# Attention of a transformer layer on one core: the last P·V products of a head issued together, its output copied out one exponential earlier, and extra matmuls of ones in the prologue

## The reference, cut to what matters

```python
qkv = x @ w_qkv + b_qkv                     # q, k, v: 16 heads of 16
q, k = rope(q), rope(k)
attn = softmax(q @ k.T / 4)                 # 2048 x 2048 for each of 4 x 16 heads
out = (attn @ v) @ w_out + b_out
x = layernorm(x + out)
gate, up = x @ w_gate.T / 127, x @ w_up.T / 127
x = layernorm(x + (silu(gate) * up) @ w_down.T / 127)
```

## Time and profile before

| | us |
|---|---|
| median of 3 runs | 2866.97 |
| the profiled execution, its own time | 2870.14 |
| its span | 2868.1 |
| PE busy | 2811.7 |
| VectorE (DVE) busy | 2702.9 |
| ScalarE (ACT) busy | 2591.9 |
| GpSimd (POOL) busy | 1416.7 |

### The profile page before, as it was taken

How to read it: one execution, slowest core, us unless ns; L and a number is a source line. 1 busy time by engine, 2 the same in 40 slices (tenths; PEclk the granted TensorE clock), 3 DMA queues, 4 the chain that set the end, 5 groups by cost and what they waited for, 6 DMA issues and landing times. The chain is left out here.

```text
span 2868.1 us, 70575 instructions
## 1 busy us (share of the span) xinstructions
PE 2811.7 (98%) x27022; PEld 862.5 (30%) x27022; DVE 2702.9 (94%) x3088; ACT 2591.9 (90%) x4778; POOL 1416.7 (49%) x4133
## 2 busy tenths in 40 slices
PE   8989999999999999999999999999999999999998
PEld 4531222222222222222222222222222222246665
DVE  7989999999999999999999999999999999947777
ACT  5756999999999999999999999999999999976555
POOL 7851444444444444444444444444444444436553
PEclk9978999999999999999999999999999999999999
DMA  5431111111111111111111111111111111233431
GB/s 194 142 116 28 36 35 36 35 36 35 35 35 35 34 35 36 35 36 36 35 35 35 36 35 35 35 35 36 35 35 36 35 35 35 70 90 92 118 96 38
DMA packets 121519, 146.56 MB, mean 51 GB/s; under 512 B 52832, under 2 KB 87520, under 8 KB 121180
## 3 DMA queue, kind: packets, MB, share of 16 engines
q1 hardware_dynamic: 120892, 142.02, 17.0%
q10 hardware_dynamic: 288, 0.01, 0.0%
HBM read 106.30 MB, written 35.13 MB: 49 GB/s over the span
## 5 line engine op out<-in xcount | busy, mean ns | idle before, releaser
L102 DVE TENSOR_REDUCE tile_max<-s_ps 128x1 f32<-128x1024 f32 (+1 forms) x2048 | 2282.4, 1185 | 8.8 <-PE s_ps L91 2.8
L1063 ACT ACTIVATE probs<-st_ps 128x512 f32<-128x512 f32 x4096 | 2202.2, 601 | 71.0 <-PE st_ps L942 41.1
L953 PE MATMUL o_ps<-probs,kept_v 128*17 128x256 f32 x16384 | 1283.1, 385 | 25.7 <-ACT sums L1032 25.7
L91 PE MATMUL s_ps<-k,q 64*128 64x512 f16 x4096 | 1266.2, 386 | 11.0 <-DVE tile_max L102 9.2
L942 PE MATMUL st_ps<-q,k 64*128 64x512 f16 x4096 | 1249.5, 382 | 1.1 <-ACT probs L1063 0.8
L1198 POOL TENSOR_TENSOR larger<-spared 128x256 f32<-128x256 f32 x1107 | 342.8, 310 | 675.6 <-ACT spared L1038 598.5
L953 PEld LDWEIGHTS o_ps<-probs,kept_v 128*17 128x17 f32 x16384 | 273.6, 95 | 852.2 <-ACT probs L1063 445.6
L942 PEld LDWEIGHTS st_ps<-q,k 64*128 64x128 f16 x4096 | 256.1, 94 | 902.0 <-ACT probs L1063 842.3
L1207 POOL TENSOR_TENSOR spared<-spared,larger 128x256 f32<-128x256 f32 x984 | 318.4, 324 | 81.9
L1200 POOL TENSOR_SCALAR larger<-larger 128x256 f32<-128x256 f32 x1107 | 261.4, 236 | 96.8
L91 PEld LDWEIGHTS s_ps<-k,q 64*128 64x128 f16 x4096 | 250.2, 94 | 50.4 <-DVE tile_max L102 46.5
(11 more groups left out here) (119 smaller groups left out, 1625.3 us busy)
## 6 DMA issues: line engine op xcount, KB each, us to landing
q<-q_parts SPq DMA_DIRECT2D x193, 128.0 KB
k<-k_parts SPq DMA_DIRECT2D x193, 128.0 KB
x_t<-in_x_t SPq DMA_DIRECT2D x16, 512.0 KB, 7.2
q_parts<-parts SPq DMA_DIRECT2D x32, 256.0 KB, 2.6
k_parts<-parts SPq DMA_DIRECT2D x32, 256.0 KB, 2.6
heads_out<-sums SPq DMA_DIRECT2D x256, 32.0 KB, 2.1
kept_v<-heads_out SPq DMA_DIRECT2D x16, 512.0 KB, 6.1
kept_v<-inverses_out SPq DMA_DIRECT2D x32, 256.0 KB
```

Of the source, the lines that this page charges most:

```text
L91: mm = pe.matmul(s["s_ps"][g % 2][:, j * BANK:(j + 1) * BANK], s["q"][h % 2][rows, r // KW * P:(r // KW + 1) * P], s["k"][h % 2][rows, at: ...
L102: dve.tensor_reduce(s["tile_max"][h % 2][:, r // KW, r % KW:r % KW + 1], s["s_ps"][g % 2][:, columns], AX.X, ALU.max).then_inc(s["s_read"], 1)
L953: mm = pe.matmul(o_ps[c * 32:c * 32 + VM, at:at + HALF], t["kept"][:, h, kt, :], probs[(h * KT + kt) % RING][:, c * BANK + at:c * BANK + a ...
L1063: act.activation(probs[(h * KT + kt) % RING][:, c * BANK:(c + 1) * BANK], st_ps[n % ST][:, :], ACT.Exp, scale=scale).then_inc(exp_done, 1)
```

## The change

`LAST_V = 1` replaces `ODD_LAST`. In iteration 1 of a head, PE now issues both halves of key tile 15 of the head before, behind both `scores_t` of that iteration; iteration 2 has no `times_v`, and its two `scores_t` both stand in their usual place. All other iterations keep their order. ScalarE copies the sums out behind exponential 3 in place of 4. In the prologue PE issues three matmuls of `ones` with `ones` (128 x 128 float32 each, all 128 rows) behind each tile's scores, into `st_ps[2]`, which nothing reads before `scores_t(2)` overwrites it; PE waits once for `ones` to be set. VectorE's `clear` moves from behind tile 18 to behind tile 16.

```diff
-    ODD_LAST = range(EXPS // 2)
+    LAST_V = 1
...
+            def busy():
+
+                for i in range(3):
+                    pe.matmul(st_ps[ST - 1][:, 0:P], w["ones"][:, :], w["ones"][:, :], start=True, stop=True)
+
+            pe.wait_ge(all_ones, 1)
             for g in range(EARLY + 2, MAXES + LEAD):
                 scores(g, 0)
                 scores(g, 1)
+                busy()
                 if g == MAXES // 2:
...
-                    odd_last = h + 1 < HEADS and n in ODD_LAST
+                    odd_last = h + 1 < HEADS and n not in (LAST_V, LAST_V + 1)
                     if not odd_last:
                         scores_t(h, 2 * n + 1)
                     before, half = divmod(n - 3, 2)
                     if before >= 0:
                         times_v(h, before, half)
-                    elif h > 0:
+                    elif h > 0 and n <= LAST_V:
                         times_v(h - 1, KT + before, half)
+                        if n == LAST_V:
+                            times_v(h - 1, KT - 1, 1)
                     if odd_last:
                         scores_t(h, 2 * n + 1)
...
-                    if e == QC and h > 0:
+                    if e == QC - 1 and h > 0:
                         drain(h - 1)
...
                 maximum(g)
+                if g == MAXES // 2:
+                    clear()
                 if g == MAXES // 2 + 2:
-                    clear()
                     dve.wait_ge(bias_done, 1)
```

## The result

The changed kernel takes **2886.02 us** (median of 14 runs, 2878.59 to 2894.21) against 2867.61 for the kernel before (14 runs): a ratio of 1.0061, 95% interval 1.0053 to 1.0069. It is slower by 18 us; the forecast was 2883. The sum was right to 3 us, but two of its terms were not: the boundary cost half of what was forecast, the prologue twice as much in the median of its own experiment (+8.3 against +4.0) and four times as much in the profiled execution (+17.6). The profiled execution took 2890.22 us, its span is 2888.3.

A forecast was written before the change was run, and what follows sets the result against it. VectorE was taken to set the pace of attention. Heads +11.8 and prologue +4.0 gave +15.8 us, 2885.9 against the profiled execution and 2883 against the median; range 2857 to 2892.

The forecast's parts named there:

- Step 1, the delay of iteration 2's tile: Head boundary: iteration 2's tile comes 0.70 us later against a lead of 0.30, so VectorE waits 0.40.
- The 0.13 at iteration 4: Head boundary: VectorE's wait before iteration 4's maximum, 0.14 with 0.01 behind it, goes with PE's stall.
- Step 1, the part that returns: Each head's iteration 12: a larger lead cuts VectorE's wait from 0.11 to about 0.03, returning 0.08 us.
- The lower bound, 7: Head boundaries: the least total loss over 62 heads, +0.11 us each, if the whole 0.11 returns and the wait is 0.36.
- my 0.19: Head boundary: net loss of +0.18 to +0.19 us a head, +11.8 us over 62 heads.
- Step 2, the copy: ScalarE's copy-out one exponential earlier: waits at most 0.1 us, covered by spare time, costed at zero.
- Step 3, the ones: Prologue: three matmuls of ones per tile make PE the bound and lift its clock; prologue +4.0 us, bounds -3 and +9.
- 5 x 0.11: Prologue tile on PE at full clock: the part for the float32 records of ones, within 1.30 us a tile.
- the 5 us of low clock: Prologue: PE stays at low clock 5 us behind 189.5, 2.5 tiles at 2.4 us, costing +3.0.
- Rival C: Prologue: the clock stays at half in spite of the ones, 36 tiles x 1.2 = +43, 2920 us; chance 0.07.
- The other two terms: Prologue: bias product with clear and add saves 1.9 us; head 0's first maxima at full clock save 1.2.
- the 0.19 us that PE waits in the prologue: Prologue before the change: at half clock PE was read as waiting 0.19 us for VectorE per tile.

The follow-up runs named there:

- real data: The kernel with the ones and the moved clear alone, its three prologue matmuls taking v kept in SBUF in place of ones: 2882.93 us, ratio 1.0044.
- the ones alone: Prologue ones and moved clear only, head boundary as in the kernel before: 2876.22 us, ratio 1.0029 against the kernel before.
- Boundary alone: New order at the head boundary and early copy only, prologue as in the kernel before: 2873.46 us, ratio 1.0019 against the kernel before.
- one matmul: One matmul of ones behind each prologue tile in place of three: 2881.04 us, ratio 1.0037 against the kernel before.
- the free rows: Float16 matmuls on rows 64 to 127 beside the prologue's score matmuls, in place of ones, clear moved: 2864.75 us, ratio 0.9988 against the kernel before.

## Why the prediction was right, step by step

**Direction and sum.** Forecast +15.8, measured +18.4. The point on which the direction rested held: VectorE, not PE, sets the pace, so a stall removed from PE is worth only what VectorE waited for it, and a tile made late is paid for as far as it goes beyond the lead. That the sum came within 3 us is luck in part: the heads came out 6 us cheaper than forecast and the prologue 4 (in the median of its own experiment) to 14 dearer (in the profiled execution), and the two misses partly cancel.

**Step 1, the delay of iteration 2's tile.** 0.70 forecast; 1.54 - 0.86 = 0.68 measured. VectorE's wait was 0.35, not 0.40: the maximum started 0.41 behind its second matmul (973.12 to 973.53), not the 0.45 that I took from iteration 4. With 0.41 the lead is 0.34, and 0.68 - 0.34 is the wait. Why iteration 4 has the longer distance is not shown. The 0.13 at iteration 4 came back as forecast.

**Step 1, the part that returns: mis-sized.** I gave back 0.08 at iteration 12; 0.12 came back, and only 0.04 of it there. I read the 0.86 between the starts of iterations 10 and 11 as VectorE's own work (a half tile and a reciprocal) and did not look at it. It held a wait of 0.08: the changed kernel does the same in 0.78. With the smaller wait, the net is +0.10 a head in place of +0.19, 5.8 us in place of 11.8. The lower bound, 7, was also too high. The order without the early copy shows where my 0.19 stood between the ends: nothing comes back there, and it costs +0.26.

**Step 2, the copy.** Costed at zero, and as part of the change it waits for nothing. But it isn't worth zero: without it the new order is 12 us slower still.

**Step 3, the ones: right in kind, mis-sized twice.** PE did become the bound of the prologue. A tile took 1.40 us, not 1.30. The term "5 x 0.11" is the one that was too small: the first of the six records starts at 216.73, the second only 0.21 later, and from there they are 0.11 apart to the last at 217.39. The way in (0.30) and the way back (217.39 to 217.59, 0.21) are as forecast.

```profile
216.94 0.39 PE L983 MATMUL st_ps<-ones 128*128 128x128 f32 x2
...
217.39 0.28 PE L983 MATMUL st_ps<-ones 128*128 128x128 f32 x1
```

By the 56 ns a record that the Trainium skill (TensorE: Matmul & The Clock Gate, "Wait — 56ns, not 53.3ns?") gives for bf16, VectorE would have ruled this stretch; the float32 records are 0.11 apart at full clock here, and it did not.

The larger miss is the 5 us of low clock: it was 28 in the profiled run of the changed kernel, 27 with real data and 11 in that of the ones alone. Rival C, to which I gave 0.07, came true for the first eleven intervals of the changed kernel's profiled run. The other two terms held: from the starts of the maxima, the bias product with `clear` and the addition came to -1.7 (forecast -1.9), the start of attention to -1.2 (forecast -1.2). Against the 1.18 of before, eleven intervals at 2.54 are +15.0 and 25 at 1.40 are +5.5, together +17.6, as measured. With the forecast's 11.8 for the heads the median would have stood at 2892, the edge of the range. A reading that nothing hung on was wrong too: the 0.19 us that PE waits in the prologue stands before every second tile, not before each (a row of x4 holds two).

**What the parts add up to.** Boundary alone +6.3, prologue alone +8.3: 14.6 against 18.4. The fastest runs differ by just the boundary (2878.59 - 2872.43 = 6.2); the medians also by how long the clock stayed low: 7 of 14 runs of the changed kernel lie over 2889, 3 of 11 runs of the ones alone over 2882. The mean granted clock of each run bears this out. It is 0.997 or 0.998 in the four runs of the changed kernel under 2880 and 0.993 in the five over 2890; an estimate from these two is 26 us less at half clock, ten tiles at 1.14 less, 11.7 us; the two groups lie 11 to 16 apart. With the ones alone it is 0.997 in the four fastest and 0.993 to 0.995 in the three over 2882. What makes the clock rise later in one run than in another is not shown.

## What to carry to other kernels

Moving work on an engine that isn't the bound is not free: add up, slot by slot, by how much it delays the next thing that the bounding engine waits for, and compare this with the lead there, which double buffering caps (0.30 us forecast before iteration 2, 0.34 measured). Look at starts, not at idle time: waits shorter than the overlap of two instructions show in no idle figure, and an interval with a small extra instruction in it can hide another. Filler work that shall lift PE's clock must fit beside the real work even at the low clock, since the time of the rise varied from run to run: here it fits on the rows of the array that the real work leaves free.

## What the runs showed of the hardware that was not expected

A PE that is busy throughout does not lift its clock by that alone: 75.7 us of float16 matmuls on rows 0 to 63, with 0.24 us of idle in all, stayed at 0.50 (1.2 GHz), while pairs on both halves brought 1.00 (2.4 GHz) 4.9 us behind the first one, and with the same pairs it stayed there while PE was busy for 27.87 of 39.00 us. The Trainium skill (TensorE: Matmul & The Clock Gate, "What's actually happening") says that activity releases the throttle; the pairs agree with it, the matmuls on half the rows do not, and there the measurement decides.

With the ones, on all rows but with holes at each switch to the scores and back, the clock stayed low for 11 to 28 us, with real data as with ones. In four of the five profiled runs in which it rose more than 10 us into the prologue (the changed kernel, real data, one matmul, the free rows), it rose during the bias product of 256 columns or 0.7 us behind it; with the ones alone, the fifth, it rose 8 us before that product. The same product did not raise it in the kernel before or with three more matmuls on half the rows. Whether the holes at the switches held it back was not isolated and stays open. The whole array in float32 between score matmuls of 64 rows in float16 costs about 0.3 us at full clock over the plain slots, in three parts of 0.1: 0.30 in place of 0.22 to the first record, 0.21 in place of 0.11 to the second, and 0.21 in place of 0.11 back to the scores.
